# A Strassen-type adaLN + LoRA-mixture kernel on one core: new setup, all blocks of base_W prepared ahead of the first product

## The reference, cut to what matters

```python
# x (128, 64, 1024), cond (128, 128), all float32
h = gelu(cond @ W0 + b0); h = gelu(h @ W1 + b1)
att = softmax(h @ W2 + b2)                     # (128, 8)
agg_w = einsum('bk,koi->boi', att, weight)     # a 64 x 64 mixing matrix for each of the 128 samples
agg_b = att @ bias_k
y = einsum('boi,bih->boh', agg_w, x) + agg_b[:, :, None]
base = einsum('bsd,od->bso', y, base_W)        # (1024, 1024) weight
w_dense = normalized top-2 of softmax(y @ router_W.T)   # 8 experts
mid = einsum('bsd,edr->bser', y, lora_A) * w_dense[..., None]
out = x + base + 2 * einsum('bser,erd->bsd', mid, lora_B)
```

## Time and profile before

| | us |
|---|---|
| median of 3 runs | 1001.0 |
| the profiled execution: its time | 1002.59 |
| its span, first to last instruction | 1000.8 |
| setup: start to the first product of pair 0 | 64.43 |
| pair 0: its first product to the first of pair 1 | 30.23 |

### The profile page before, as it was taken

The page is one execution under the profiler, slowest core; times in us unless marked ns, Lnnn a source line. Parts: engine busy times, 40 slices in busy tenths (PEclk is TensorE's granted clock), DMA queues, the critical chain, the costliest instruction groups (busy, mean ns, idle before and its releaser), DMA issues.

```text
span 1000.8 us, 18047 instructions
## 1 busy us (share of the span) xinstructions
PE 967.0 (97%) x5882; PEld 893.4 (89%) x5882; DVE 684.9 (68%) x1550; ACT 210.4 (21%) x428; POOL 334.7 (33%) x249
## 2 busy tenths in 40 slices
PE   4589999999999999999999999999999999999998
PEld 2589999999999999999999999999999999999996
DVE  5367667766766767676676767667776766777674
ACT  4241112221211222121122212121221212122120
POOL 6353332233333223333322333332233333223331
PEclk9799999999999999999999999999999999999999
DMA  7532343332334333233433333343333234333311
GB/s 242 139 129 72 114 135 109 112 131 99 106 113 134 110 113 128 99 105 113 134 109 120 122 102 103 113 134 117 117 117 106 99 113 134 117 122 112 108 54 58
DMA packets 75602, 115.35 MB, mean 115 GB/s; under 512 B 48280, under 2 KB 48664, under 8 KB 75424
## 3 DMA queue, kind: packets, MB, share of 16 engines
q1 hardware_dynamic: 75440, 113.02, 35.4%
q10 hardware_dynamic: 144, 2.10, 0.5%
HBM read 79.41 MB, written 35.68 MB: 115 GB/s over the span
## 4 chain that ended last, share of the span: by engine, by line
PE 95%; DVE 2%; issue 1%; SPq 1%; DMA 0%; ACT 0%; DVEq 0%; ACTq 0%
PE pc L564 17%; PE pa L575 13%; PE pb L575 13%; PE y_ps L534 12%; PE pa L578 10%; PE pb L578 10%; PE pd L564 9%; PE pd L596 4%; PE pc L596 4%; DVE w_lo L805 1%; PE pd L586 1%; DMA mixk_raw<-in_L_cond_weight 0%; DVE mixk L830 0%; DVE out_sb L926 0%; PE y_ps L484 0%
## 5 line engine op out<-in xcount | busy, mean ns | idle before, releaser
L411 POOL TENSOR_TENSOR out_sb<-out_sb,u 128x512 f32<-128x512 f32 x96 | 136.6, 1452 | 215.5 <-DVE u L989 215.5
L534 PE MATMUL y_ps<-mix_w,x_sb 128*128 128x128 f32 x1024 | 197.2, 277 | 11.7 <-issue 11.7
L534 PEld LDWEIGHTS y_ps<-mix_w,x_sb 128*128 128x128 f32 x1024 | 169.9, 193 | 22.7 <-issue 11.9
L379 POOL TENSOR_TENSOR ya<-ya 128x512 f32<-128x512 f32 x32 | 42.7, 1334 | 404.4 <-DVE ya L866 404.4
L866 DVE TENSOR_TENSOR ya<-y_ps,bias_sb 128x512 f32<-128x512 f32 x128 | 87.9, 687 | 46.2 <-PE y_ps L534 43.1
L564 PE MATMUL pc<-w_hi,s_hi 128*128 128x512 f32 x256 | 105.7, 413 | 0.0
L575 PE MATMUL pa<-w_hi,a_hi 128*128 128x376 f32 x256 | 101.3, 396 | 2.2 <-DVE w_lo L937 1.4
L564 PE MATMUL pc<-w_hi,s_lo 128*128 128x512 f32 x256 | 100.7, 393 | 0.0
L564 PE MATMUL pc<-w_lo,s_hi 128*128 128x512 f32 x256 | 100.0, 391 | 0.0
L575 PE MATMUL pa<-w_hi,a_lo 128*128 128x376 f32 x256 | 86.0, 336 | 0.0
L575 PE MATMUL pa<-w_lo,a_hi 128*128 128x376 f32 x256 | 85.8, 335 | 0.0
(11 more groups left out here) (189 smaller groups left out, 2419.7 us busy)
## 6 DMA issues: line engine op xcount, KB each, us to landing
x_sb<-in_x SPq DMA_DIRECT2D x64, 512.0 KB, 5.1
out_sb<-in_x SPq DMA_DIRECT2D x64, 512.0 KB, 4.7
out<-out_sb SPq DMA_DIRECT2D x64, 512.0 KB, 2.7
w_raw<-in_L_ffn_base_W SPq DMA_DIRECT2D x4, 1024.0 KB, 11.4
bias_sb<-bias_rows SPq DMA_DIRECT2D x64, 64.0 KB, 5.2
agg_rows<-agg ACTq DMA_DIRECT2D x1, 2048.0 KB, 7.6
mix_w<-agg_rows SPq DMA_DIRECT2D x128, 16.0 KB, 3.7
mixk_raw<-in_L_cond_weight SPq DMA_DIRECT2D x4, 128.0 KB
```

Of the source, the lines that this page charges most:

```text
L379: nc.gpsimd.tensor_tensor(y_block(0, 1), y_block(0, 1), y_block(0, 0), ALU.subtract).then_inc(s3_set, 1)
L411: nc.gpsimd.tensor_tensor(o, o, u2[:, :], ALU.add).then_inc(done, 1)
L534: mm = nc.tensor.matmul(y_ps[q % 2][:, j * P:(j + 1) * P], x_sb[m][:, c * P:(c + 1) * P], mix_w[m][:, :], start=True, stop=True)
```

## The change

Only the setup and the first pair change; from pair 1 on every engine's program is as before. In words:

- base_W is loaded by ScalarE's queue from the start, in four contiguous tiles, rather than by SP's behind the small loads.
- `weight` is loaded once, into 8 partitions, and `mixing_kernels` works in plain float32 on 8 rows: the splits of L716, L830, L341 and L343, the fourfold attention matrix and the memsets for them are gone. Its output goes to `pa`. `take_agg` reads and writes in another order (four contiguous values, then a stride).
- The first pair's mixing matrices are copied from `agg` in SBUF (not by way of DRAM); the bias rows come ahead of them. `agg` is still written to DRAM by ScalarE's queue for all later tiles.
- lora_A is loaded by one DMA (64 rows of 8 KB), transposed by 16 TensorE instructions and split by ScalarE and VectorE.
- T3 is a GpSimd subtraction too. The blocks' order is B11, B22, T1, B21, T3, T2, T4; four banks in rotation, two for T4. B11 is transposed amid the small network and `mixing_kernels`, B22 before the first mixing, the other 20 groups after it and ahead of the first product. VectorE takes those 20 (`first_body`) after `split_low(S3, 0)`.
- The first product waits only for B11, B22, router_W and lora_A; P2, P7 and P6 of pair 0 wait for their blocks.
- In pair 0 the mixing of pair 1 stands one product later (P2, P7, P6, P5 in place of P1, P2, P7, P6), and ScalarE's and VectorE's orders for pair 0 are written out anew.

The diff, cut to its core:

```diff
+    GROUPS = (B11, B22, T1, B21, T3, T2, T4)
-        w_ps = [pa[:, 0:BANK], pa[:, BANK:], pb[:, 0:BANK], pb[:, BANK:], pc[:, :], pd[:, :]]
-        mlp_ps = [w_ps[4], w_ps[5]]
+        w_ps = [pb[:, 0:BANK], pb[:, BANK:], pc[:, :], pd[:, :]]
+        agg_ps = [pa[:, 0:BANK], pa[:, BANK:]]
+        mlp_ps = y_ps
+        def group_ps(g):
+            return w_ps[g % 4] if g < NG - HALF else w_ps[2 + g % 2]
...
         @block.sync
-            for q in range(P // Q):
-                sp.dma_start(mixk_raw[q * Q:(q + 1) * Q:KS, :],
-                             weight.rearrange("k o i a -> k (o i a)")).then_inc(mix_in, 16)
-            for n, (g, d) in enumerate(((0, 0), (0, 1), (1, 0), (1, 1))):
-                sp.dma_start(w_raw[:, rows, cols], base_rows[:, rows, cols]).then_inc(w_in[n], 16)
+            sp.dma_start(mixk_raw[:, :], weight.rearrange("k o i a -> k (o i a)")).then_inc(mix_in, 16)
+            sp.dma_start(bk_sb[:, :], bias_k).then_inc(bk_in, 16)
+            sp.dma_start(la_raw2[:, :], lora_a.rearrange("e (c d) r -> (e c) (d r)", c=NC)).then_inc(la_in, 16)
...
-            for c in range(NC):
-                sp.dma_start(la_raw[:, c, :, :],
-                             lora_a[:, c * P:(c + 1) * P, :].rearrange("e p r -> p e r")).then_inc(la_in, 16)
+            sp.wait_ge(bias_out, 16)
+            for m in range(2):
+                mixing_bias(m, m)
+            sp.wait_ge(agg_act, 4)
+            sp.wait_ge(agg_dve, 4)
+            for m in range(2):
+                mixing_weights(m, m, agg)
...
         @block.gpsimd
+            nc.gpsimd.tensor_tensor(t1_raw[:, :], w_raw[2][:, :], w_raw[0][:, :], ALU.subtract).then_inc(t_set, 1)
+            nc.gpsimd.tensor_tensor(w_raw[2][:, :], w_raw[2][:, :], w_raw[3][:, :], ALU.subtract).then_inc(t_set, 1)
+            nc.gpsimd.tensor_tensor(t2_raw[:, :], w_raw[3][:, :], t1_raw[:, :], ALU.subtract).then_inc(t_set, 1)
+            pool.wait_ge(w_tr, HALF)
+            nc.gpsimd.tensor_tensor(w_raw[0][:, :], w_raw[1][:, :], t2_raw[:, :], ALU.subtract).then_inc(t_set, 1)
...
         @block.tensor
+                if g >= NG - HALF:
+                    pe.wait_ge(w_lo_set, g - 1)
+                elif g >= 4:
+                    pe.wait_ge(w_lo_set, g - 3)
...
-                nc.tensor.matmul(y_ps[n % 2][:, :], att_parts[:, :], mixk[:, n * BANK:(n + 1) * BANK],
+                nc.tensor.matmul(agg_ps[n % 2], att_t[:, :], mixk_raw[:, n * BANK:(n + 1) * BANK],
...
+            for n in range(8):
+                mixing_kernels(n)
+                if n in (1, 3):
+                    w_group(n // 2 + 2)
+            for r in range(R):
+                tr = nc.tensor.transpose(pa[:, r * E * NC:(r + 1) * E * NC], la_raw[:, r, :],
+                                         ident[0:E * NC, 0:E * NC])
+            for g in range(HALF, 2 * HALF):
+                w_group(g)
             for q in range(4):
                 for j in range(HALF):
                     mix_chunk(0, q, j)
-            for g in range(HALF * (B22 + 1), NG):
+            for g in range(2 * HALF, NG):
                 w_group(g)
-            pe.wait_ge(w_lo_set, NG + 1)
+            pe.wait_ge(w_lo_set, 2 * HALF)
+            pe.wait_ge(rw_lo_set, 1)
             pe.wait_ge(la_lo_set, 1)
...
+                def mixed_in(place, j):
+                    q = place - first(p)
+                    if not last(p) and 0 <= q < 4:
+                        mix_chunk(p + 1, q, j)
...
         @block.scalar
+            load_w(0)
+            load_w(2)
             nc.scalar.activation(warm[:, :], nc.const_aps.tensor(0.0, (P, 1)), ACT.Gelu)
+            load_w(3)
+            load_w(1)
...
         @block.vector
+            def first_body():
+                for g in range(2 * HALF, NG):
+                    take_w(g)
+                dve.wait_ge(p2_mm, 1)
+                route_logits(0, pa[:, SLOG])
+                route_choice(0)
+                route_weigh(0, pa[:, SMID])
+                split_low(S2, 0)
+                split_low(S1, 0)
+                add_bias(1, 0)
...
```

More of the change, by code:

```diff
@@ L84, in adaln_ffn_kernel @@
             op_lo.append(place(f"{o}_lo", BANK, f32r)[1])
-        out_sb = [[place(f"out_sb{k}{s}", D)[1] for s in range(2)] for k in range(2)]
+        out_at, out_sb = [], []
+        for k in range(2):
+            pair = [place(f"out_sb{k}{s}", D) for s in range(2)]
+            out_at.append(pair[0][0])
+            out_sb.append([t for _, t in pair])
         p1_at, p1 = place("p1", BANK + SD)
@@ L600, in body @@
             def body(p, k):
-                mixing = not last(p)
+                def mixed_in(place, j):
+                    q = place - first(p)
+                    if not last(p) and 0 <= q < 4:
+                        mix_chunk(p + 1, q, j)
                 wait_operand(A11, p)
@@ L629, in body @@
                         mm.then_inc(p2_mm, 1)
-                    if mixing:
-                        mix_chunk(p + 1, 1, j)
+                    mixed_in(1, j)
                 wait_operand(S3, p)
-                if not first(p):
+                if first(p):
+                    pe.wait_ge(w_lo_set, 22)
+                else:
                     pe.wait_ge(out21_p74, p)
@@ L641, in body @@
                         mm.then_inc(p7_mm, 1)
-                    if mixing:
-                        mix_chunk(p + 1, 2, j)
+                    mixed_in(2, j)
                 wait_operand(S2, p)
-                if not first(p):
+                if first(p):
+                    pe.wait_ge(w_lo_set, NG)
+                else:
                     pe.wait_ge(out21_up, p)
@@ new lines, in make_u2, with add_p12, add_p5 @@
+            def make_u2(p):
+                dve.wait_ge(p6_mm, p + 1)
+                dve.wait_ge(p1_kept, p + 1)
+                if not first(p):
+                    dve.wait_ge(u2_in21, p)
+                nc.vector.tensor_tensor(u2[:, :], pd[:, :], p1[:, 0:BANK], ALU.add).then_inc(u2_ready, 1)
+            def add_p12(p, k):
+                dve.wait_ge(res_in[k][0], 8 * (p - k) + 16)
+                add_into(k, 0, 0, pa[:, BASE], out11_p12)
+            def add_p5(p, k):
+                dve.wait_ge(p5_mm, p + 1)
+                dve.wait_ge(u2_in22, p + 1)
+                add_into(k, 1, 1, pc[:, :], out22_p5)
@@ new lines, in add_up11_p74, with first_body @@
+            def add_up11_p74(p, k):
+                dve.wait_ge(up11_mm, p + 1)
+                dve.wait_ge(out11_p12, p + 1)
+                add_into(k, 0, 0, pd[:, :], out11_up)
+                dve.wait_ge(u2_in21, p + 1)
+                add_into(k, 1, 0, pb[:, BASE], out21_p74)
+            def first_body():
+                for g in range(2 * HALF, NG):
+                    take_w(g)
+                dve.wait_ge(p2_mm, 1)
[5 more added lines that the diff above has]
+                add_bias(1, 0)
+                split_low(A22, 0)
+                split_low(S4, 0)
+                add_p7(0, 0)
+                add_bias(1, 1)
+                split_low(A11, 1)
+                make_u2(0)
+                split_mid(0)
+                add_bias(1, 2)
+                split_low(S3, 1)
+                add_p12(0, 0)
+                add_p5(0, 0)
+                add_bias(1, 3)
+                split_low(A12, 1)
+                add_side_b(0)
+                add_up11_p74(0, 0)
@@ L963, in body @@
                     add_bias(p + 1, 0)
-                if not first(p):
-                    finish_odd(p - 1, 1 - k)
+                finish_odd(p - 1, 1 - k)
                 split_low(A22, p)
```

377 lines of the change are left out of this document (146 added, 231 removed).

## The result

The changed kernel takes 1007.20 us, the median of 7 runs (1005.54 to 1008.04), against 1000.99 of the kernel before beside it (7 runs, 999.86 to 1003.63). The ratio is 1.0058, with a 95% interval of 1.0048 to 1.0069. It is 6.2 us slower, where 988.0 was forecast. The profiled execution took 1005.62, at the low end of its runs, over a span of 1003.9; that of before had taken 1002.59, at the high end, over 1000.8.

A forecast was written before the change was run, and what follows sets the result against it. TensorE was taken to bound from pair 1 on, so only the stretch before counted: 52.2 + 0.8 + 28.6 = 81.6 against 94.66, 13.0 less, hence 988.0 us against 1001.0. Forecast 985 to 991 (0.54), range 982 to 994.

The forecast's parts named there:

- (2): mixing_kernels: the clock rises at about 16 us, and agg is complete at 23.4, bounds 21.0 and 28.
- (1): Small network: its loads lose 0.9 us beside base_W, at most 5.3, and mixing_kernels starts at about 11.3.
- Rival (c): Small network starves beside base_W and the kernels run at half clock: 4 to 5 us more, 992.5; chance 0.13.
- A: The time from the start of the span at which agg is complete, forecast at 23.4 us.
- (3): Fetch of the first mixing matrices: held up behind agg_rows' 2 MB write, they land at A + 8.
- A + 6: Mixing matrices' landing by the skill's round robin: small DMAs pass within a few large packets; not used in the sum.
- the trace's rule: Mixing matrices' fetch: small DMAs stand until agg_rows has passed, 6.5 us with start-up, as an empty microsecond suggested.
- (4): First mixing, 16 chunks: 5.8 us, ending at A + 13.8 = 37.2, with the last add_bias at 37.95.
- (5): The 20 groups after the first mixing: first product 14.2 us after the last add_bias, at 52.2 against 64.43.
- rival (b): The clock stays low throughout the groups ahead of the first product: 992.2 us; chance 0.13.
- (6): Pair 0: 28.6 us plus 0.8 for the lower clock; pair 1 starts at 81.6, against 94.66.
- (d): Pair 0's new order leaves VectorE behind, costing every pair: slower than before, 1006 at 0.6 us a pair; chance 0.03.

The follow-up runs named there:

- Experiment 1: The changed kernel with base_W's four DMAs issued by SyncE's queue behind the small loads, not by ScalarE's from the start: 1003.71 us, ratio 1.0029 to the kernel before.
- Experiment 4: The changed kernel with mixing_kernels' matmuls on 128 rows, 120 of them zeros, in place of 8: 1000.91 us, ratio 0.9994 to the kernel before.
- Experiment 3: The changed kernel with agg's copy to DRAM on SyncE's queue behind the first mixing matrices: 1000.95 us, ratio 0.9996 to the kernel before.
- experiment 6: The changed kernel with VectorE taking 8 groups ahead of A12's low part and T3's ahead of S3's: 1005.87 us, ratio 1.0054 to the kernel before.
- experiment 7: The changed kernel with side_b added and routed ahead of A12's low part at pair 0's end: 1005.89 us, ratio 1.0050 to the kernel before.
- experiment 9: The changed kernel with all seven separately tried edits together, and the bias rows' write on ScalarE's queue: 982.64 us, ratio 0.9810 to the kernel before.
- 10: The kernel of experiment 9 with all 20 groups ahead of the first product again: 987.12 us, ratio 0.9853 to the kernel before.
- experiment 5: The changed kernel with T3's, T2's and T4's groups moved between P1's and P2's products: 1001.37 us, ratio 1.0006 to the kernel before.

## Why the prediction was wrong, step by step

The prediction failed at (2), where the clock was let rise in `mixing_kernels`, and at (1), where 0.9 us was put down for the small loads beside base_W. The runs showed a clock that stayed at its lower level through all eight kernels (5.3 us) and kernels that started 5.45 us late; together that is 10.7 of the 16.0 by which the profiled execution missed its forecast.

(1) **Mis-sized: the small network.** I let the small loads lose 0.9 us beside base_W; the softmax's start moved by 6.6, outside even my bound of 5.3. I had reasoned that a piece of 2 KB makes a small packet wait for little. But the seven loads are needed one after the other, and the last, issued at 3.96, took 8.9 us. Between 4 and 6 us base_W's queue had 365 of the 552 packets and 93.6% of the engines' time. Experiment 1 puts the GELU back at 4.72. Rival (c) was right in this half. `mixing_kernels` started at 16.75, not at 11.3: 5.45 us.

(2) **Failed: the clock in `mixing_kernels`.** I let it rise at 16, as it had in the transposes of the earlier trace rows, and gave no thought to the matmuls' filling 8 rows. TensorE was busy all of each 2 us from 18 to 34, and still every kernel took its half-clock 1.7 us. From the kernels' start to `agg` it took 17.4 where I had 12.1: 5.3 us. My bound of 28 for A did hold "the lower clock all through", but from a start at 11.3. Experiment 4 shows the cause in the number of rows. Rival (c)'s other half was right too, and its price, 4 to 5 us for both halves, was less than half of the 10.7 that they cost.

(3) **Right, but 1.8 too short.** The matrices were held up behind `agg_rows`: A + 9.8, not A + 8. Experiment 3 shows it. `agg_rows`' rows were through at 39.9, A + 5.8, even a little sooner than my 6.5; the mis-sized term is the 1.5 for the small ones' own packets, which took 3.6 (39.9 to 43.5). "No small packet" held until 38 us; 35 passed beside the last 48 large ones. By the Trainium skill's round robin at packets ("DMA: Bandwidth & Descriptors", Queues, rings and completion order) I had worked out A + 6. The measured time speaks for the trace's rule and against my A + 6. It doesn't speak against the skill's: there I had taken every row of 16 KB for a packet, but 128 rows over 16 engines are 8 an engine if they are spread evenly, fewer than the 9 to 17 descriptors that it gives a packet, so that the whole of an engine's share could be one. No run here tests that.

(4) **Nearly right, 1.0 too short.** The first mixing took 6.34 for 5.8; another 0.5 went between its end and the last `add_bias` (1.22, not 0.75), since VectorE was late with a low part.

(5) **Mis-sized: the groups.** The first product came 16.4 after the last `add_bias`, not 14.2. VectorE's first group began after 3.5, not 1.9: S3's low part took 1.75 us and A12's 1.20, where the same operation takes 0.68 while GpSimd stands idle (A12's in experiment 6). GpSimd ran its sums from 51.58 to 56.20; A12's low part ended 0.55 after the first of them, S3's 0.56 after the second. Group low parts, which read one operand from PSUM, kept their 0.67 beside the same sums. The Trainium skill says just this ("SBUF — State Buffer", SBUF: two separate sides): a VectorE operation with two SBUF inputs and a GpSimd one that reads SBUF exclude each other, and the loser blocks. The trace agrees. The cost didn't end there: TensorE stood idle 3.7 us for a bank, and between 56 and 60 us the clock was down, in windows with the columns of the earlier trace rows:

```profile
56.00:58.00 2.00, 2.00 (x12) 1.85 (x11) 2.00 (x4) 1.12 (x2) 1.92 (x3) 0.51 0.40 128
58.00:60.00 2.00, 2.00 (x14) 2.00 (x13) 1.63 (x4) 1.43 (x4) 1.63 (x1) 0.63 0.51 163
60.00:62.00 2.00, 2.00 (x17) 1.46 (x16) 2.00 (x4) 2.00 (x5) 0.00 (x0) 1.00 0.02 7
```

Experiment 6 takes back 1.2 of it. Apart from these 4 us the groups' clock was as I took it. The rule of the Trainium skill that rival (b) named ("TensorE: Matmul & The Clock Gate", Part 4: in transpose mode the full clock doesn't engage) is not borne out here: the clock came back at about 59 us, with nothing but transposes behind it, and 8 of them had taken 1.04 at 50.10.

(6) **Right for pair 0, incomplete behind it.** 28.92 against 28.6 and 0.8. But VectorE, with more written ahead of it at the end of pair 0, began `side_b` at 94.55, 1.9 after P4's end, and that cost pair 1 another 0.9 (experiment 7). This is rival (d)'s mechanism, once and not in every pair.

The account at the first product: 5.45 + 5.3 + 1.8 + 0.5 + 0.5 + 2.2 = 15.7, and 52.2 + 15.7 is the 67.88 of the trace. Pair 0 gave back 0.5 and pair 1 took 0.9. That makes 16.0 from the 989.6 of the forecast execution to 1005.62. The last 3.2 are the medians: I had set the median 1.6 below the profiled execution, and it lay 1.6 above it. The traces don't explain that part.

The links form one chain, so each delay moved all that came after it, and the range took the rivals one at a time and left out (b) with (c). For the kernel to come out slower I had only (d), a cost repeated in every pair. It needed none: six errors on the way to the first product, two of over 5 us and four small ones, all in one direction, made 15.7 and so took the forecast gain of 13.0 and more.

The question that the change put, all blocks ahead of the first product, has its own answer: 4.5 us lost (experiments 9 and 10), 2.8 by the trace and 5.8 by the medians in the changed kernel itself (experiment 5). The rest of the new setup is good when its delays are taken out: 982.64.

Open: why the matmuls on 8 rows stay slow, beyond that they do; how much of each starved load is lost to the packets' order and how much to memory; and the 3 us between the difference of the profiles and that of the medians, which is also in the gains of the experiments. base_W on ScalarE's queue but issued later was not tried.

## What to carry to other kernels

A bulk load that is moved to an idle queue isn't moved past the small loads, it is put beside them: a chain of small dependent loads has to land first, and a small transfer that someone waits for should be issued before a large one. Where it can't be, the other queue was the better place here: the bias rows' write took 6.0 us beside the loads and 14.9 behind them. Fewer bytes and fewer splits can be outweighed if the matmul that replaces them fills 8 of 128 rows; look at durations, since such a stretch appears as a fully busy engine. And work that alternates between TensorE and VectorE through a few banks belongs between matmuls that wait for nothing, not in a block of its own.

## What the runs showed of the hardware

**Rows and the clock.** Float32 matmuls of 512 columns on 8 rows ran for 17 us, with two groups of transposes between them, at 1.71 us each, the pace of the lower clock. The windows' column for the granted clock said 1.00 all the while; its first lower value stands at 42 to 44 us. In experiment 1's trace it says 1.00 even over the first mixing, whose 16 chunks took 5.98 (in experiment 9, at the full clock, 8 of them take 2.02). So ahead of its first lower value the column isn't to be trusted, and durations must be read. Filled up with zeros to 128 rows, from the third on they ran at twice the pace (3.78 for two, then 1.88).

**Small transfers beside large ones.** 16 KB in 128 pieces of 128 B took 2.3 us with no large one in flight and 7.0 beside a transfer of 2 MB in 16 KB rows on the other queue; 4 KB took 2.6 and 8.9 beside 2 KB rows. Beside the 16 KB rows no small packet moved in the first 80 large ones. Beside the 2 KB rows the packets were mixed (187 of the 552 between 4 and 6 us were the other queue's), and the small load was slow all the same.

**VectorE beside GpSimd.** The same 128x512 operation with two SBUF inputs took 0.68 us while GpSimd stood idle, and 1.20 or 1.75 beside its sums; with one input in PSUM it kept 0.67 beside them.
